# Linear attention: the rotation of half a head by transfers between partitions, with the signs in the sine table

## The reference

```
q = (hidden_states @ Wq.T + bq)   # k and v the same way
cos, sin: tables of position and frequency, 16 frequencies, repeated for the two halves of a head
def _rotate_half(x): x1, x2 = halves of the last dimension; return concatenate((-x2, x1))
q = q * cos + _rotate_half(q) * sin
k = k * cos + _rotate_half(k) * sin
p = (q / norm(q)) @ rand_matrix.T;  qp = concatenate([sin(p), cos(p)]) / sqrt(32)   # kp from k the same way
kv = sum over heads of kp (outer) v, for each token;  out = qp @ kv;  out @ Wo.T + bo
```

## Time and profile before

| | us |
|---|---|
| median of 3 runs | 2363.11 (2361.16 to 2364.78) |
| the profiled execution | 2363.24 |
| its span in the profile | 2361.5 |
| PE busy | 2062.1 (87%) |
| DVE busy | 1227.2 (52%) |
| ACT busy | 746.9 (32%) |
| POOL busy | 220.9 (9%) |

### The profile page before, as it was taken

One profiled execution on the slowest core, in us unless ns is written; L12 is line 12 of the kernel. 1 busy time (PEld: TensorE's weight loads), 2 busy tenths in 40 slices (PEclk: granted clock), 3 DMA queues, 4 the chain that ended last, 5 costly groups with the idle time before them and its releaser, 6 DMA issues. The chain is left out here.

```text
span 2361.5 us, 29596 instructions
## 1 busy us (share of the span) xinstructions
PE 2062.1 (87%) x12078; PEld 987.3 (42%) x12078; DVE 1227.2 (52%) x2281; ACT 746.9 (32%) x1163; POOL 220.9 (9%) x164
## 2 busy tenths in 40 slices
PE   5885669697975499989999899999998999999998
PEld 3553233334343344434444444444444444444443
DVE  5554364757643455463666265644565356623332
ACT  4562231324341112322235223432244223511211
POOL 3630202120200000000000010001000000000000
PEclk7886769797966599999999999999999999999999
DMA  7224030302021222322111111111111111122321
GB/s 258 83 72 167 1 58 1 58 1 58 8 52 72 81 72 98 110 87 72 45 42 59 53 46 37 63 36 63 54 55 45 54 46 54 63 90 99 116 93 68
DMA packets 90978, 158.75 MB, mean 67 GB/s; under 512 B 44182, under 2 KB 55772, under 8 KB 86108
## 3 DMA queue, kind: packets, MB, share of 16 engines
q1 hardware_dynamic: 90844, 156.86, 20.7%
HBM read 128.52 MB, written 18.87 MB: 62 GB/s over the span
## 5 line engine op out<-in xcount | busy, mean ns | idle before, releaser
L1169 PE MATMUL ps<-arena 128*128 128x512 f16 (+1 forms) x4512 | 1018.3, 381 | 22.6 <-DVE arena L1932 12.9
L1169 PEld LDWEIGHTS ps<-arena 128*128 128x128 f16 x4512 | 436.4, 99 | 542.8 <-issue 48.5
L1877 PE MATMUL ps<-arena 128*128 128x512 f16 x1536 | 349.0, 383 | 29.5 <-DVE arena L1923 16.3
L1877 PEld LDWEIGHTS ps<-arena 128*128 128x128 f16 x1536 | 147.4, 98 | 207.4 <-issue 29.4
L1899 ACT ACTIVATE arena<-ps,arena 128x512 f32<-128x512 f32 x128 | 87.6, 684 | 362.4 <-PE ps L1169 362.1
L1932 DVE SCALAR_TENSOR_TENSOR arena<-arena,ps 128x512 f32<-128x512 f32 x128 | 87.8, 686 | 210.1 <-ACT arena L1899 209.5
L2486 ACT ACTIVATE arena<-ps 128x1024 f32<-128x1024 f32 (+3 forms) x128 | 90.1, 704 | 253.7 <-PE ps L2395 253.6
L2591 DVE CAST arena<-arena 128x1024 f16<-128x1024 f32 (+3 forms) x128 | 66.6, 520 | 149.8 <-ACT arena L2486 147.7
L2557 DVE TENSOR_REDUCE arena<-ps 128x2 f32<-128x256 f32 (+3 forms) x128 | 99.5, 819 | 65.1 <-PE ps L2339 65.1
L1960 DVE SCALAR_TENSOR_TENSOR arena<-ps,arena 128x512 f32<-128x512 f32 x64 | 44.0, 687 | 139.6 <-PE ps L1877 139.4
L1941 DVE SCALAR_TENSOR_TENSOR arena<-ps,arena 128x512 f32<-128x512 f32 x128 | 95.7, 748 | 39.5 <-PE ps L1169 39.3
(11 more groups left out here) (265 smaller groups left out, 2446.7 us busy)
## 6 DMA issues: line engine op xcount, KB each, us to landing
arena<-wug_dram SPq DMA_DIRECT2D x128, 512.0 KB, 3.3
arena<-wd_hi_dram SPq DMA_DIRECT2D x16, 1024.0 KB, 5.0
arena<-wd_lo_dram SPq DMA_DIRECT2D x16, 1024.0 KB, 7.2
arena<-arena SPq DMA_DIRECT2D x144, 64.0 KB, 2.1
wug_dram<-arena SPq DMA_DIRECT2D x4, 2048.0 KB, 15.4
arena<-_attn_hidden_states_dram SPq DMA_DIRECT2D x4, 1024.0 KB, 12.4
arena<-in_L_ffn_W_up_dram SPq DMA_DIRECT2D x8, 512.0 KB, 4.4
arena<-in_L_ffn_W_down_dram SPq DMA_DIRECT2D x4, 1024.0 KB, 7.7
```

Of the source, the lines that this page charges most:

```text
L1169: ins = pe.matmul(out, left[a](c), right[b](c), start=(at == 0), stop=(at == 3 * n - 1))
L1877: ins = pe.matmul(k.ps[:, bank, :], act[x][:, slot, cols], wd[y][:, f, :], start=(f == 0 and m == 0), stop=(f == 7 and m == 2))
```

## The change

The rotation of a half head becomes eight transfers for each part. For each group of 16 partitions, SP copies `qf` of the neighbouring group (p ^ 16) into `ang`, slot z % 2. The matrix `rot` leaves the constants, and the sign of the rotated half moves into the sine table. PE no longer rotates. DVE's first rope operation reads `ang` in SBUF in place of PSUM bank 4, and waits for the 8 x 16 counts of part z's transfers, on one of two semaphores. SP waits for `qf[z]`, for rope z - 2 (which read the same slot of `ang`), and for the first two parts for the low features of the chunk before. The two new semaphores take the place of `b_rot` and `wd_in3`, for which the fourth load of the down weights counts on `wd_in0`.

```diff
-    rot = np.zeros((P, P), np.float32)
-    for m in range(P):
...
-    parts = [("ident", ident), ("had", had), ("rot", rot), ("cos", np.cos(ang)),
-             ("sin", np.sin(ang)), ("key", key), ("iota", iota), ("causal", causal),
+    parts = [("ident", ident), ("had", had), ("cos", np.cos(ang)),
+             ("sin", np.where(r % 32 < 16, -1.0, 1.0).astype(np.float32)[:, None] * np.sin(ang)), ("key", key), ("iota", iota), ("causal", causal),
...
-            sp.dma_start(k.wd_nat[:, o % 3, :], d["L1_ffn_W_down"][o * P:(o + 1) * P, :]).then_inc(s[f"wd_in{o}"], 16)
+            sp.dma_start(k.wd_nat[:, o % 3, :], d["L1_ffn_W_down"][o * P:(o + 1) * P, :]).then_inc(s[f"wd_in{o % 3}"], 16)
...
-        e.wait_ge(s[f"wd_in{o}"], 16)
+        e.wait_ge(s[f"wd_in{o % 3}"], 16 * (o // 3 + 1))
...
-    def rotate(z):
-        pe.wait_ge(s["b_qf"], 6 * new + z + 1)
-        need(pe, s["b_rope"], 6 * new + z)
-        pe.matmul(k.ps[:, ROT_BANK, :], k.c["rot"], k.qf[:, z, :], start=True, stop=True).then_inc(s["b_rot"], 1)
...
-            if y in ROT_AT:
-                rotate(ROT_AT.index(y))
...
+def halves_sync(k, sp, i):
+    s = k.s
+    for z in range(6):
+        sp.wait_ge(s["b_qf"], 6 * i + z + 1)
+        need(sp, s["b_rope"], 6 * i + z - 1 if z >= 2 else 0)
+        need(sp, s["b_f_lo"], 6 * i if z < 2 else 0)
+        for p in range(0, P, 16):
+            sp.dma_start(k.ang[p:p + 16, z % 2, :], k.qf[p ^ 16:(p ^ 16) + 16, z, :]).then_inc(s[f"b_turn{z % 2}"], 16)
...
     def rope(z):
-        e.wait_ge(s["b_rot"], 6 * new + z + 1)
+        e.wait_ge(s[f"b_turn{z % 2}"], 128 * (3 * new + z // 2 + 1))
         e.wait_ge(s["b_cos"], 6 * new + z + 1)
-        V.link(e.tensor_tensor(k.qf[:, z, :], k.ps[:, ROT_BANK, :], k.c["sin"], ALU.mult))
+        V.link(e.tensor_tensor(k.qf[:, z, :], k.ang[:, z % 2, :], k.c["sin"], ALU.mult))
         e.tensor_tensor(k.qr[:, z, :], k.qr[:, z, :], k.qf[:, z, :], ALU.add).then_inc(s["b_rope"], 1)
...
             for i in range(NCH):
+                halves_sync(k, sp, i)
                 b_sync(k, sp, i)
```

More of the change, by code:

```diff
@@ L86 @@
 nat_in0 nat_in1 nat_turned wt_hi wt_lo had_done had_hi had_lo
-wd_in0 wd_in1 wd_in2 wd_in3 wd_scaled wd_mixed wd_step wdo_lo wdo_out
+wd_in0 wd_in1 wd_in2 wd_scaled wd_mixed wd_step wdo_lo wdo_out
 ss_chain vec_turned vec_set up_scale
@@ L93 @@
 n_var n_ln n_std n_norm n_h n_turned n_hi n_lo
-b_v_done b_v_in b_v_out b_vr b_qk_done b_qf b_cos b_rot b_rope b_sq b_nsum b_n2 b_ln b_n b_r b_proj b_p b_spread b_y
+b_v_done b_v_in b_v_out b_vr b_qk_done b_qf b_cos b_turn0 b_turn1 b_rope b_sq b_nsum b_n2 b_ln b_n b_r b_proj b_p b_spread b_y
 b_reduced b_feat b_f_hi b_f_lo b_ks b_ksg b_qs b_s b_mask b_pv b_ot_hi b_ot_lo b_out b_res b_bo
@@ L1188 @@
 PROJ_BANK = (2, 3)
-ROT_BANK = 4
 LENGTH_BANK = 7
```

## The result

The changed kernel takes **2372.24 us** (median of 6 runs, 2371.56 to 2375.54) against 2362.47 for the kernel before on the same chip (2361.16 to 2364.78): a ratio of **1.0042, 95% interval 1.0029 to 1.0055**. It is slower by about 10 us. The forecast of 2360.0 missed the direction; the time lies in the range, where the rival "SP's queue becomes the bound" put it (2376, or +10 before its clock term).

The account below looks back on a forecast made before the run. It took PE as the bound in chunks 1 to 3 and a four-engine chain in chunk 0. Chunks +3.7 - 4.3 - 2.7 - 2.7, clock +2.2 + 1, constants -0.2 made -3.0 us: 2360.0, range 2352 to 2376.

Parts of the forecast that it names:

- SP's queue becomes the bound: Rival: at 0.64 us per issue, eight take 5.1 us, ropes follow SP's queue; +10, with the clock +13, 2376; chance 0.22.
- I take 0.50, which is also the middle: Price in us of one transfer issue on SP, from eight loads into 16 partitions, with ends 0.36 and 0.64.
- +3.7 had been forecast: Chunk 0 at 0.50 us per issue: rope 5 at 284.5 to 284.9 instead of 281.18, before any clock loss.
- It decides from about 0.56 us per issue: Issue price from which the queue makes the kernel slower: chunk 0's +5.5 eats the other chunks' -2.7 - 1.5 - 1.5.
- Chunks 1 to 3: +0.2 each: At 0.64 us per issue, the loss in each later chunk, with PE standing at the lengths, before the clock.
- The clock term of 1 us for the three: Tails of chunks 1 to 3: longer waits for lengths 4 and 5 lower PE's clock, +1 together, bound 0 to 4.
- +2.2 for a slow projection: Chunk 0: PE idles 3 us ahead of a length, so projection 4 starts at low clock, 4.94 us for 2.77.
- So a shift there is a shift of the end: What follows the touched stretches begins when the lengths are in, so their gain or loss passes whole to the end.
- Issue time is nothing: Rival: issuing costs almost no time, a part is turned 2.5 us after its `qf`; -15 us, 2348; chance 0.05.
- The constants' -0.2: Set-up: the constants shrink by 64 of 1043 KB, at most -0.3 us, taken as -0.2.
- If DVE waits for transfers in every part, the queue rival is right: Sign in the profile after: DVE waiting on every part's transfers would mean SP's issue queue sets the pace.
- That of chunk 1 about 4 us nearer to the stretch's start: Sign in the profile after: chunk 1's last length comes about 4 us nearer to its stretch's start than before.

Follow-up runs that it names:

- e_four: Changed kernel with four transfers of 32 partitions per part in place of eight of 16, without the exchange of half heads: 2346.67 us.
- e_two: Changed kernel with features reordered in the set-up, so the exchange is two transfers of 64 partitions per part: 2350.15 us.
- e_best: Changed kernel with two transfers of 64 partitions, the feature order made when the turned weights are written: 2343.06 us, ratio 0.9919 to the kernel before.
- e_dram: Changed kernel with the same eight transfers of 16 partitions read from a weight array in DRAM, leaving out the rotation's values: 2351.58 us.
- e_again: The changed kernel once more, unaltered, for a second profile: 2374.8 us.
- e_keep: Changed kernel with all eight transfers, plus PE's 24 rotations as spare work whose result nobody reads; DVE waits for both: 2372.2 us.
- e_none: Changed kernel without any rotation: no transfers, DVE's product reads `qf` itself: 2341.94 us.
- e_rest_pe: Changed kernel with chunks 1 to 3 turned by PE's matmul again, only chunk 0 by the eight transfers: 2371.41 us.

## Why the prediction was wrong, point by point

**The failed step: "I take 0.50, which is also the middle".** The price of an issue was a choice between a row alike in shape (0.36 with its gap), one alike in memories (0.64), and a middle that eight loads from DRAM had shown. It was 0.589 and its gap, 0.63 to 0.65 a piece. The kernels with 16, 32 and 64 partitions show about the same price (0.589; 0.591 in e_four; 0.563 and 0.557 in e_two and e_best), and e_dram that from DRAM it is lower (0.420). The text named the steadiness of 0.597 over 144 transfers as evidence for the rival and still took the middle of unlike rows. By the rival's own working chunk 0 gives +9.3, and from `qf` 0 to the last product it measured +9.2 in both executions. Its stretch grew by 7.6 in the first profile, which had the faster first projections, and by 9.4 in e_again, where +3.7 had been forecast, or +5.9 with the clock's term. "It decides from about 0.56 us per issue" fits as far as it was tried: at 0.65 the kernel is slower, in e_dram it is faster.

**"Chunks 1 to 3: +0.2 each"** for that price was too low. They measured +3.3, +2.1 and +2.5, and +0.9, +2.5 and +1.5 in e_again. The clock term of 1 us for the three was mis-sized, where the three lost 7.9 us in all, and 4.8 in e_again. In e_keep, at PE's clock of before, they are +0.3, +1.0 and +0.3, near what the queue alone was worked out to give. The changed kernel shows it between two executions: chunk 1 took 52.23 us at a granted clock of 0.79, and 49.81 at 0.88 in e_again:

```profile
361.00:411.00 50.00, 40.48 (x365) 16.24 (x357) 23.48 (x49) 7.81 (x12) 12.58 (x12) 0.88 0.14 33
```

I had the clock fall in tails only. In fact it fell in the busy stretch too, from the wait of 2.90 us ahead of length 1 on: I had let PE go on in that stretch whatever the ropes did. Of chunk 0's clock loss, +2.2 for a slow projection, about 1.0 came: the two projections behind length 1 took 6.47 us together, where the same 24 matmuls take 5.37 in e_best.

**"So a shift there is a shift of the end"** was the assumption under the whole sum, and it doesn't hold to a few us. The stretches lose 15.4 us in the profile, the span 8.3. The stretches don't fill all the time from 252 to 644: between them 3.4 us came back (0.1 ahead of the first; the first turn of chunk 3 stands 11.9 us later, not 15.4). At the first load of a down weight (L2666 before, L2664 after) the shift is 13.2 us (743.61 for 730.41), and 8.4 at 1610.70 for 1602.34, from where it stays. These 4.8 us come back in three places between, 1.6 to 1.7 us each. At the first, PE's timeline has the same 48 matmuls after the same wait; the first fence is the kernel before, the second the changed one:

```profile
729.99 12.30 PE L1169 MATMUL ps<-arena 128*128 128x512 f16 x48 [1.44 <-DVE arena L1576]
```

```profile
743.18 10.53 PE L1163 MATMUL ps<-arena 128*128 128x512 f16 x48 [1.44 <-DVE arena L1574]
```

12.30 or 10.53 us, in the table by stretch at a granted clock of 0.83 (730.4 to 740) and 1.00 (743.6 to 753). Work that the change doesn't touch met the clock at another level. The other executions bear it out. e_again has the same three steps, from 14.8 us behind at the first of these loads to 10.0 at 1612.33. From the first to the second load of a down weight before took 159.3 us and e_keep 159.5, but the changed kernel 157.7 (e_again too), e_none 157.6 and e_best 157.5. e_none has no transfers at all, so it is not they that do it. In its profiled execution e_keep came to the first load 4.5 us ahead of the changed kernel and got none of the three, which cost it 5.1: that is why its shorter stretches don't show in its time. e_rest_pe came there 6.0 us later than before and reached the load that answers to 1602.34 at 1600.17: it got back 8.2 us, in such steps. Which of the two durations a place gets, and what in a change decides it, stays open. So do the smaller shifts: the 3.4 us between the stretches, and 1.3 lost from 644 to 744.

**Right:** landing (2.1 taken, 2.0 measured), and the equal price of DVE's product with both sources in SBUF, 693 ns as in the earlier trace rows:

```profile
L1581 DVE TENSOR_TENSOR arena<-arena x24: 679/693/694, 262.3 to 633.6; 128x512 f32<-128x512 f32 x24
```

Right too was the gain that PE's rotations hide. "Issue time is nothing" had -2.4, -4.5, -4.1 and -4.1 for the four chunks; e_none measured -4.1, -6.0, -5.0 and -3.5, and in total -19.6 us (the ratio's 0.83%) for the -15 worked out. The mechanism of the whole sum (what PE gives up against what the queue takes) held. The constants' -0.2 is within the noise: the first projection starts 0.1 us earlier. The range, 2352 to 2376, held the time as its upper end was built from the 0.64 row.

**The signs foretold.** "Eight issues of a part in 3.9 to 4.0 us, 5.1 for the rival": 5.1 between products. "If DVE waits for transfers in every part, the queue rival is right": in 18 of 24. "PE idle ahead of lengths 1 and 4": 4.32 and 4.03, and also ahead of 5 (3.16). "The last length of chunk 0 near 289": 291.26. "That of chunk 1 about 4 us nearer to the stretch's start": it stands 1.8 us farther.

## What to carry to other kernels

Price a serial issue by a row with the same source and target memories, not by the shape of the transfer, and compare the issues of one part with the pace of the chain that waits for them: eight made 5.1 us against a floor of 3.7, four or two disappeared under it. So before moving an exchange of partitions to the DMA queues, choose the order of the features so that it needs few transfers, and make that order where a write happens anyway; failing that, share the issues between two queues. When a sum is made for stretches with a changing TensorE clock, keep a couple of us per stretch for the clock, and a few more for untouched work behind them; and profile a kernel twice before reading a difference of 2 us in one stretch.

## What was not expected of the hardware

- Arena to arena, an issue on SP's queue takes 0.56 to 0.59 us whether it moves 16, 32 or 64 partitions of 2 KB; from DRAM, 16 partitions of 2 KB take 0.42. ACT's queue asks 0.61 and runs in parallel.
- In chunk 1 PE lost twelve matmul instructions and its parts waited for transfers: the granted clock fell from 0.95 to 0.79 (0.88 in a second execution), and only 1.5 us of busy time were saved. Neither alone lowered it: with the twelve gone but no such waits (e_best, 365 recorded instructions) PE was busy for 37.90 us at 0.95, and with the waits but spare rotations on PE (e_keep) the clock was 0.95 too. The changed kernel, with 373 recorded, was busy for 42.62.
- Work far behind a change (48 matmuls at 730 us) took 12.30 or 10.53 us, by the clock that it met. Such steps of 1.6 to 1.7 us, three in the changed kernel and some five in e_rest_pe, are as large as the differences that one looks for.
